# Row-norm deviations as exp(-0.5*ln(v)) on ScalarE, weights centred once, norm steps and their neighbours moved

## What is computed

```python
def _layernorm(x, axis=-1, eps=1e-05):
    m = jnp.mean(x, axis=axis, keepdims=True)
    v = jnp.var(x, axis=axis, keepdims=True)
    return (x - m) / jnp.sqrt(v + eps)
# attention, 16 heads of 8: q = x @ Wq.T + bq, v = x @ Wv.T + bv, buckets from 6 hyperplanes
scores = jnp.einsum('bhsd,bhtd->bhst', q, q) / jnp.sqrt(jnp.float32(E))
same = (b_hs[:, :, :, None] == b_hs[:, :, None, :]).astype(scores.dtype)
attn = jax.nn.softmax(scores * (NB - 2 + same), axis=-1)
# feed-forward, 128 -> 512 -> 512 -> 512 -> 128, ternary weights
h = jax.nn.silu(_tlin(x, w1_w, w1_s)) * _tlin(x, w2_w, w2_s)
h = gelu(_tlin(h, h1_w, h1_s)); h = gelu(_tlin(h, h2_w, h2_s)); return _tlin(h, w3_w, w3_s)
# layer
x = x + _layernorm(attention(_layernorm(x)))
x = x + _layernorm(ffn(_layernorm(x)))
```

## Time and profile before

| | us |
|---|---|
| median of three executions (lowest to highest) | 1383.29 (1378.63 to 1386.29) |
| span of the profiled execution | 1378.0 |
| busy: PE / DVE / ACT / POOL | 1223.5 / 1225.7 / 1084.6 / 1221.7 |
| share of the span: PE / DVE / ACT / POOL | 89% / 89% / 79% / 89% |
| POOL: 128 subtractions L980 | 1138.7 |
| POOL: 48 powers L970 and 48 products L972 | 48.7 and 9.6 |
| ACT: 512 exponentials L1032 | 509.0 |
| ACT: 196 table loads (L1032 88, L1150 31, L1155 31, L1160 29, L1127 16, L1025 1) | 251.5 |
| mean granted clock of TensorE | 0.975 |

### The profile page before, as it was taken

The page is one execution under the profiler, slowest core; times in us unless marked ns, Lnnn a source line. Parts: engine busy times, 40 slices in busy tenths (PEclk is TensorE's granted clock), DMA queues, the critical chain, the costliest instruction groups (busy, mean ns, idle before and its releaser), DMA issues. The chain is left out here.

```text
span 1378.0 us, 19641 instructions
## 1 busy us (share of the span) xinstructions
PE 1223.5 (89%) x5302; PEld 500.2 (36%) x5394; DVE 1225.7 (89%) x3837; ACT 1084.6 (79%) x1573; POOL 1221.7 (89%) x259
## 2 busy tenths in 40 slices
PE   3666799999989999998989999998999999898897
PEld 1211234343333434333343434433343433333343
DVE  4988999999999999999999999999999999999420
ACT  2344778979797988979798897979798897979852
POOL 2699999999999999999999999999999998999810
PEclk9877999999999999999999999999999999999998
DMA  3563445444544455455544544454454535453100
GB/s 104 154 182 112 132 111 154 127 130 120 147 120 118 132 134 141 109 140 125 131 133 124 142 123 132 133 139 129 114 136 128 145 98 146 120 135 102 40 8 8
DMA packets 89470, 167.37 MB, mean 121 GB/s; under 512 B 18192, under 2 KB 54160, under 8 KB 89360
## 3 DMA queue, kind: packets, MB, share of 16 engines
q1 hardware_dynamic: 89252, 165.82, 44.6%
q10 hardware_dynamic: 108, 0.30, 0.1%
HBM read 150.59 MB, written 15.47 MB: 121 GB/s over the span
## 5 line engine op out<-in xcount | busy, mean ns | idle before, releaser
L980 POOL TENSOR_TENSOR logits<-max_row,logits 128x4096 f32<-128x4096 f32 x128 | 1138.7, 8915 | 65.6 <-DMA max_row<-max_scratch 41.0
L808 DVE CUSTOM_DVE_ANT_0 logits<-s_bank,coeff 128x512 f32<-128x512 f32 x1024 | 692.5, 676 | 0.0
L1032 ACT ACTIVATE logits<-logits 128x1024 f32<-128x1024 f32 x512 | 509.0, 1048 | 44.8 <-POOL logits L980 43.6
L758 DVE TENSOR_SCALAR coeff<-brow,bcol 128x516 bf16<-128x516 bf16 x1024 | 485.2, 474 | 36.8 <-PE s_bank L550 31.2
L550 PE MATMUL s_bank<-mov_stack,stat_stack 128*128 128x512 bf16 x932 | 324.8, 393 | 42.4 <-DVE rowmax L808 31.7
L570 PE MATMUL aux_bank<-logits,v_pad 128*32 128x512 f32 x2048 | 255.3, 618 | 39.8 <-ACT logits L1032 38.9
L701 PE MATMUL f_bank<-hid_b,h_sb 128*128 128x512 f32 x512 | 249.0, 594 | 0.9
L690 PE MATMUL f_bank<-hid_a,h_sb 128*128 128x512 f32 x512 | 246.1, 592 | 0.1
L550 PEld LDWEIGHTS s_bank<-mov_stack,stat_stack 128*128 128x128 bf16 x1024 | 93.2, 99 | 317.7 <-DVE rowmax L808 177.8
L690 PEld LDWEIGHTS f_bank<-hid_a,h_sb 128*128 128x128 f32 x512 | 96.0, 190 | 80.6 <-issue 69.3
L701 PEld LDWEIGHTS f_bank<-hid_b,h_sb 128*128 128x128 f32 x512 | 95.0, 190 | 80.8 <-issue 70.9
(11 more groups left out here) (101 smaller groups left out, 911.5 us busy)
## 6 DMA issues: line engine op xcount, KB each, us to landing
max_row<-max_scratch SPq DMA_DIRECT2D x128, 512.0 KB, 4.2
brow<-bucket_scratch SPq DMA_DIRECT2D x63, 522.0 KB, 6.3
mov_stack<-q_scratch SPq DMA_DIRECT2D x192, 96.0 KB
stat_stack<-q_scratch SPq DMA_DIRECT2D x189, 96.0 KB
max_scratch<-rowmax_T SPq DMA_DIRECT2D x512, 1.0 KB
q_scratch<-q_parts SPq DMA_DIRECT2D x16, 384.0 KB, 4.6
x_in<-in_x SPq DMA_DIRECT2D x16, 256.0 KB, 3.1
q_scratch<-q_parts SPq DMA_DIRECT2D x16, 256.0 KB, 5.1
```

Of the source, the lines that this page charges most:

```text
L758: nc.vector.tensor_scalar(coeff[:, k % 3, :].rearrange("p (r n) -> p r n", r=ROW_RUNS), brow[:, h // 4 % 2, h % 4, :, 0:RUN], bcol[:, b % ...
L808: nc.vector.tensor_tensor_reduce(out=logits[:, ring(b, k), :], in0=tile_bank(k)[:], in1=coeff[:, k % 3, 0:SEQ], scale=float(E) ** -0.5, sc ...
L980: nc.gpsimd.tensor_tensor(tiles, max_row[:, m % 2].unsqueeze(2).broadcast_to([P, GROUP, ST, SEQ]), tiles, ALU.subtract).then_inc(below_max ...
L1032: nc.scalar.activation(logits[:, first:first + 2, :], logits[:, first:first + 2, :], ACT.Exp, scale=-1.0).then_inc(probs_done, 1)
```

## The change

The reciprocal deviations of all four norms come from ACT, as exp(-0.5*ln(v + eps)), and the table that is named for both functions takes the place of the softmax's exp table; it is loaded by an instruction of its own behind each pair of Silu or Gelu. POOL's powers and products, `Sqrt` and DVE's reciprocal go. The means of x and y aren't subtracted any more: Wq, Wv, W1 and W2 are multiplied once by I - 1/128 on PE and copied back by ACT. The norm of the attention's output keeps its mean, and its bias is made on DVE in slot 29. Slots move. The diff, cut to its core:

```diff
@@ -54,6 +54,8 @@
 PADDED = ROW_RUNS * RUN
 ROW_PITCH = ROW_RUNS * RUN_PITCH
 EPS = 1e-5
+CONSTS = 5
+EXP_LOG_TABLE = "natural_log_exp_and_others"
...
 SILU_SLOTS = (42, 48)
-MULTIPLY_SLOTS = (48, 48, 52, 52)
-OUTPUT_SLOTS = (100, 101, 104, 104)
+MULTIPLY_SLOTS = (45, 48, 52, 52)
+OUTPUT_SLOTS = (100, 103, 105, 105)
...
 PV_LAGS = (36, 36, 38, 38)
-COPY_LAG = 35
+COPY_LAG = 34
...
 LATE_X_STATS_SLOT = 33
-X_MOMENTS_SLOT = 24
+X_MOMENTS_SLOT = 21
 LATE_X_MOMENTS_SLOT = 37
-X_PREPARE_SLOT = 26
+X_PREPARE_SLOT = 25
 LATE_X_PREPARE_SLOT = 38
-X_RSTD_SLOT = 40
-LATE_X_RSTD_SLOT = 47
...
 XNT_COPY_SLOT = 53
-XNT_SLOT = 57
+XNT_SLOT = 58
 Q_COPY_SLOT = 57
-Q_SLOT = 59
+Q_SLOT = 61
 
-V_SLOT = 32
+V_SLOT = 33
...
 PROJ_SLOT = 25
-BITS_SLOT = 26
+BITS_SLOT = 25
...
 ATT_MOMENTS_SLOT = 25
 ATT_PREPARE_SLOT = 27
-ATT_RSTD_SLOT = 32
-ATT_NORM_SLOT = 31
+ATT_BIAS_SLOT = 29
+ATT_NORM_SLOT = 29
 RESIDUAL_SLOT = 32
-Y1_STATS_SLOT = 32
-Y1_MOMENTS_SLOT = 32
+Y1_STATS_SLOT = 33
+Y1_MOMENTS_SLOT = 34
 Y1_PREPARE_SLOT = 34
-Y1_RSTD_SLOT = 39
-Y1_NORM_SLOT = 37
+Y1_NORM_SLOT = 34
...
 END_PREPARE_SLOT = 49
-END_RSTD_SLOT = 56
 END_NORM_SLOT = 55
-Y2_SLOT = 62
+Y2_SLOT = 61
...
 FFN_LOAD_STEP = 3
-X_RES_SLOT = 44
+X_RES_SLOT = 46
...
+        centre = hid_b[:, 0, 0:P]
...
-            pe.wait_ge(consts_made, 4)
+            pe.wait_ge(consts_made, CONSTS)
+
+            for n, weights in enumerate((wq_sb, wv_sb)):
+                nc.tensor.matmul(f_bank[n][:, 0:E], centre, weights[:], start=True, stop=True).then_inc(centred_psum, 1)
...
                     last.then_inc(xnT_psum, 1)
                 if k == Q_SLOT:
                     pe.wait_ge(xnT_done, p + 1)
+                    if not begun(p):
+                        pe.wait_ge(projection_centred, 2)
                     nc.tensor.matmul(aux_bank[:], wq_sb[:], xnT[:], start=True, stop=True).then_inc(q_psum, 1)
...
                             pe.wait_ge(ynT_done, f + 1)
+                            if f == 0:
+                                pe.wait_ge(ffn_centred, 2)
...
                     pe.wait_ge(ffn_in, 16 * FFN_DMAS)
+                    pe.wait_ge(brow_done, i + 1)
+                    for n, weights in enumerate((w1_sb, w2_sb)):
+                        nc.tensor.matmul(f_bank[n][:], centre, weights[:], start=True,
+                                         stop=True).then_inc(ffn_centred_psum, 1)
...
+                if k == ATT_BIAS_SLOT:
+                    dve.wait_ge(att_rstd_done, f + 1)
+                    nc.vector.scalar_tensor_tensor(out=att_bias[:], in0=att_mv[:, :, 0], scalar=-1.0, in1=att_rstd[:],
+                                                   op0=ALU.mult, op1=ALU.mult).then_inc(att_bias_done, 1)
...
-            def finish_step(g, k):
-                if k == END_RSTD_SLOT:
-                    dve.wait_ge(end_std_done, g + 1)
-                    nc.vector.reciprocal(end_rstd[:], end_std[:]).then_inc(end_rstd_done, 1)
...
-            nc.gpsimd.memset(minus_half[:], -0.5).then_inc(consts_made, 1)
+            nc.gpsimd.memset(centre, -1.0 / E).then_inc(consts_made, 1)
             nc.gpsimd.memset(eps[:], EPS).then_inc(consts_made, 1)
-            pool.wait_ge(consts_made, 1)
+            pool.wait_ge(consts_made, 3)
             nc.gpsimd.affine_select(out=ident[:], in_=ident[:], compare_op=ALU.not_equal, fill=1.0, base=0,
                                     pattern=[[-1, P]], channel_multiplier=1).then_inc(consts_made, 1)
-            pool.wait_ge(consts_made, 4)
-            def rstd(var, shift, out_, bias, prepared, done, bias_done, n):
-
-                pool.wait_ge(prepared, n)
-                nc.gpsimd.tensor_tensor(out_[:], var[:], minus_half[:], ALU.pow).then_inc(done, 1)
-                pool.wait_ge(done, n)
-                nc.gpsimd.tensor_tensor(bias[:], shift[:], out_[:], ALU.mult).then_inc(bias_done, 1)
-
+            nc.gpsimd.affine_select(out=centre, in_=centre, compare_op=ALU.not_equal, fill=1.0 - 1.0 / E, base=0,
+                                    pattern=[[-1, P]], channel_multiplier=1).then_inc(consts_made, 1)
             def subtract(b, m):
 
                 pool.wait_ge(maxima_loaded[m % 2], 16 * (b * GROUPS // 2 + m // 2 + 1))
@@ -997,12 +1000,6 @@
...
-                    if query and k == x_slot(i + 2, X_RSTD_SLOT, LATE_X_RSTD_SLOT):
-                        rstd(x_var, x_shift, x_rstd, x_bias, x_var_done, x_rstd_done, x_bias_done, p + 2)
-                    if feed and k == ATT_RSTD_SLOT:
-                        rstd(att_var, att_shift, att_rstd, att_bias, att_var_done, att_rstd_done, att_bias_done, 2 * f + 1)
-                    if feed and k == Y1_RSTD_SLOT:
-                        rstd(att_var, att_shift, att_rstd, att_bias, att_var_done, att_rstd_done, att_bias_done, 2 * f + 2)
...
-            act.wait_ge(consts_made, 4)
-            nc.scalar.activation(table_warm[:], ident[:, 0:1], ACT.Exp)
+            nc.scalar.preload_act_table_set(EXP_LOG_TABLE)
+            act.wait_ge(consts_made, CONSTS)
             act.wait_ge(projection_in, 16 * PROJECTION_DMAS)
+            for n, weights in enumerate((wq_sb, wv_sb)):
+                act.wait_ge(centred_psum, n + 1)
+                nc.scalar.copy(weights[:], f_bank[n][:, 0:E]).then_inc(projection_centred, 1)
...
-            def prepare(mv, var, shift, ready, done, n):
-
-                act.wait_ge(ready, n)
-                nc.scalar.activation(var[:], mv[:, :, 1], ACT.Identity, bias=eps[:])
-                nc.scalar.activation(shift[:], mv[:, :, 0], ACT.Identity, scale=-1.0).then_inc(done, 1)
-
-            def normalise(dst, src, rstd, bias, done):
+            def rstd(var, scale, log, out_, ready, count, log_done, done, n):
+
+                act.wait_ge(ready, count)
+                nc.scalar.activation(log[:], var, ACT.Ln, bias=eps[:], scale=scale).then_inc(log_done, 1)
+                act.wait_ge(log_done, n)
+                nc.scalar.activation(out_[:], log[:], ACT.Exp, scale=-0.5).then_inc(done, 1)
+
+            def scale_rows(dst, src, rstd_, rstd_done, n, done):
+                act.wait_ge(rstd_done, n)
                 for t in range(ST):
-                    last = nc.scalar.activation(dst[:, t, :], src[:, t, :], ACT.Identity, bias=bias[:, t:t + 1],
-                                                scale=rstd[:, t:t + 1])
+                    last = nc.scalar.activation(dst[:, t, :], src[:, t, :], ACT.Identity, scale=rstd_[:, t:t + 1])
...
                 if k == x_slot(p, X_PREPARE_SLOT, LATE_X_PREPARE_SLOT):
-                    prepare(x_mv, x_var, x_shift, x_mv_done, x_var_done, p + 1)
+                    rstd(x_mv[:, :, 1], 1.0, x_log, x_rstd, x_mv_done, p + 1, x_log_done, x_rstd_done, p + 1)
                 if k == X_NORM_SLOT:
-                    act.wait_ge(x_bias_done, p + 1)
-                    normalise(x_in, x_in, x_rstd, x_bias, xn_done)
+                    scale_rows(x_in, x_in, x_rstd, x_rstd_done, p + 1, xn_done)
...
                 if slot == ATT_PREPARE_SLOT:
-                    prepare(att_mv, att_var, att_shift, att_mv_done, att_var_done, 2 * f + 1)
+                    rstd(att_mv[:, :, 1], 1.0, att_log, att_rstd, att_mv_done, 2 * f + 1, att_log_done, att_rstd_done, f + 1)
                 if slot == Y1_PREPARE_SLOT:
-                    prepare(att_mv, att_var, att_shift, att_mv_done, att_var_done, 2 * f + 2)
+                    rstd(att_mv[:, :, 1], 1.0, y1_log, y1_rstd, att_mv_done, 2 * f + 2, y1_log_done, y1_rstd_done, f + 1)
...
                 if slot == END_PREPARE_SLOT + TILES:
-                    act.wait_ge(end_square_done, (f + 1) * ST)
-                    nc.scalar.activation(end_std[:], end_sum[:], ACT.Sqrt, bias=eps[:],
-                                         scale=1.0 / E).then_inc(end_std_done, 1)
+                    rstd(end_sum[:], 1.0 / E, end_log, end_rstd, end_square_done, (f + 1) * ST, end_log_done, end_rstd_done,
+                         f + 1)
                 if slot == ATT_NORM_SLOT:
                     if f:
 
                         act.wait_ge(h2_done, (f - 1) * HT + 2)
-                    act.wait_ge(att_bias_done, 2 * f + 1)
-                    normalise(f_bank[OUTPUT_BANK][:].rearrange("p (t e) -> p t e", t=ST), att, att_rstd, att_bias, normed_done)
+                    act.wait_ge(att_bias_done, f + 1)
+                    for t in range(ST):
+                        last = nc.scalar.activation(f_bank[OUTPUT_BANK][:, t * E:(t + 1) * E], att[:, t, :], ACT.Identity,
+                                                    bias=att_bias[:, t:t + 1], scale=att_rstd[:, t:t + 1])
+                    last.then_inc(normed_done, 1)
                 if slot == Y1_NORM_SLOT:
-                    act.wait_ge(att_bias_done, 2 * f + 2)
-                    normalise(x_res, y1[:, f % 2], att_rstd, att_bias, yn_done)
+                    scale_rows(x_res, y1[:, f % 2], y1_rstd, y1_rstd_done, f + 1, yn_done)
                 if slot == END_NORM_SLOT + TILES:
```

(37 more changed lines are left out.)

## The result

The changed kernel takes 1446.6 us (median of 4 runs, 1438.8 to 1471.1); the kernel before 1382.5 us (4 runs). The changed kernel's run of 1471.1 us was in a slower state of the chip and is left out of the ratio. The ratio is 1.0438, with an interval of 1.0390 to 1.0487: 4.4% slower, where the prediction had 0.6% faster and a range up to 1387. The profiled execution of the changed kernel spans 1441.8 us, 63.8 more than the 1378.0 of before.

What follows compares the result with a forecast made beforehand. It took DVE as nearest to the bound. Fourteen passes of 0.55 us (7.7) plus 1.0 in the last batch gave 8.7, so 1383.3 - 8.7 = 1374.6 us; own range 1369 to 1379, overall range 1361 to 1387.

Steps and rivals of the forecast that it cites:

- Reciprocal out, bias product in: both 128x4, no difference: On DVE: swapping the reciprocal for the new bias product of equal size was taken to cost nothing.
- so I charge 0: DVE's new wait for att_rstd in slot 29: taken as covered, 0; 0.5 us a pass if that cover goes.
- Rival D: DVE's first product, three slots earlier behind Silu, waits too long and lengthens each pass: 1392 us, chance 0.08.
- rival E: Compiler adds its own table loads, two between bucket rows and Silu, delaying DVE's products: 1404 us, chance 0.05.
- the load inside ACT's wait for the rows: Exponential's table load (1.28 us) moves into ACT's wait before the bucket rows' copy, delaying that copy by 0.15 us.
- PE has the same work ahead of them as before: PE's transposes ahead of `ynT` stay in place, so `ynT` and Silu start only 0.6 us earlier; bounds 0 and 1.36.
- 5 or 6: Expected sign: POOL's wait for maxima grows to this many us a pass, from 2.6.
- 0.3 to 0.6: Expected sign: us a pass that DVE waits for ACT ahead of its first product, no longer ahead of the third.
- Rival C: No change: PE holds the transposes, or DVE's new wait in slot 45 eats the gain; 1381 us, chance 0.22.
- rival B: POOL gated the passes; waits for y, Silu, up branch and some for scores go: 20 us gained, 1363, chance 0.15.
- the last batch's 1.0: After the last accumulator: Ln and Exp save 1.2 us, table loads between Silu pairs lose 0.2; net 1.0 saved.
- DVE is nearest to the bound: Of the engines in a pass, DVE limits most: busy 76.2 of 78.7 us, waiting 2.5 us a pass.

Runs made afterwards that it cites:

- e1: Changed kernel with slot 29's bias product written as four 128x1 products of one tensor and a pointer scalar; 1361.1 us, ratio 0.9876 to the kernel before.
- e3: Kernel before plus one unread dummy 128x4 DVE product a pass in slot 32, first tensor in PSUM, other in SBUF; 1381.4 us, ratio 1.0015.
- e2: Kernel before plus one unread dummy 128x4 DVE product a pass in slot 32, both tensors in SBUF; 1467.2 us, ratio 1.0642.
- e10: e1 with the exp and log table load moved from behind the last Gelu pair to behind the bucket rows' copy; 1373.7 us, ratio 0.9942.
- e12: Kernel before with only the exponential's table load moved directly behind a pass's last Gelu pair, ahead of ACT's wait; 1368.5 us, ratio 0.9916.
- e6: e1 with the output matmuls back in their old slots 100, 101, 104, 104; 1360.4 us, ratio 0.9854 to the kernel before.
- e7: e1 with three pairs of power and product a pass put back on POOL, on constants, read by nobody; 1364.9 us, ratio 0.9888.
- e5: e1 with the first product of gate and up branch back in slot 48; 1362.4 us, ratio 0.9866 to the kernel before.
- e8: Changed kernel with the attention norm's bias made on ACT (negated mean, four 128x1 products), nothing of it on DVE; 1372.6 us, ratio 0.9937.
- e4: Changed kernel with each POOL subtraction cut into two instructions of 128x2048; 1398.9 us, ratio 1.0159 to the kernel before.

## Why the prediction was wrong

**The step that failed** is the one on DVE: "Reciprocal out, bias product in: both 128x4, no difference", and with it "so I charge 0" for slot 29. The product was sized by its elements. The trace of before has no DVE instruction with two SBUF tensors: its sums and products read one of theirs from PSUM. So the operation was one that the trace did not show, and it was to be bounded from both sides. The length that turned out to be the upper bound was in the same trace, POOL's subtraction of 8.9 us, with POOL busy 95% of the pass; but no row of before shows that DVE can be held by it, only e1 to e3 do. Sixteen stalls of up to 8.9 give up to 142 us; the 10 that came cost 78.8 (changed kernel against e1). How many came and how long they were owes to luck, to where slot 29 happens to fall: if the product fell anywhere in a subtraction, the mean stall would be 4.4 us; here it is 8.3, since slot 29 mostly falls on its first microsecond. The description ahead of the prediction says that the engines "meet only at semaphores"; e1 to e3 show that DVE and POOL also meet at SBUF, with no semaphore between them (5.58 us in the median of e2's 16 products, 0.16 in e3). The slower rivals, D and E, were other mechanisms, and neither happened.

**The cause of the sign is thus shown** from three sides: taken out of the changed kernel (e1), put alone into the kernel before (e2), and with a tensor moved to PSUM (e3).

**The gain that the prediction was about** is there once the stall is out: 1378.0 - 1363.0 = 15.0 us between the profiled spans, where 8.7 were forecast. The mechanism, the load inside ACT's wait for the rows, was right (e10 and e12) and a term was too small. The 14 passes went from 78.85 to 77.85 us (marks of e1: 184.2 to 1274.1), so 1.0 each and not 0.55; the rest after the last mark shrank from 90.1 to 88.9, 1.2 against the predicted 1.0. The term is the start of PE's transposes, which the prediction left at 631.36 because "PE has the same work ahead of them as before". But what ended PE's idle time there was ACT's norm of y, which in the kernel before ended at 631.30, 0.06 ahead of them:

```profile
629.67 1.63 ACT L1043 ACTIVATE x_res<-y,att_bias,att_rstd 128x128 f32<-128x128 f32 x4
```

This norm stands behind the table load, so it moves with it. ACT and PE in pass 7 of e1 (compare), and PE in pass 7 of e12:

```profile
619.20 1.28 ACT L1164 ACT_TABLE_LOAD   x1
620.50 0.43 ACT L1097 CAST brow<-f_bank 16x344 bf16<-16x344 f32 x1
...
626.41 0.59 ACT L1145 COPY ynT<-f_bank 128x512 f32<-128x512 f32 x1
...
630.43 1.26 ACT L1150 ACTIVATE hid_a<-f_bank,scales_sb 128x512 f32<-128x512 f32 x2
```

```profile
625.73 0.60 PE L649 MATMUL f_bank<-ident,x_res 128*128 128x128 f32 x4
```

```profile
625.41 0.60 PE L643 MATMUL f_bank<-ident,x_res 128*128 128x128 f32 x4
```

Counted from the end of the last exponential of the group before (621.81 before, 616.61 in e1, 616.20 in e12), in e1 the copy of the rows came 0.17 later, as predicted (0.15). The transposes came after 9.12 us and not 9.55, 0.43 earlier, where I had left them in place; `ynT` after 9.80 and not 10.82, and Silu after 13.82 and not 14.84, 1.02 earlier. (The medians of 13 passes are the same within 0.02.) In e1 the norm ends 2.9 us ahead of the transposes, and PE's own queue holds them. Other kernels split the 0.43. In e12, which changes the load's place alone, the transposes come after 9.22 us, 0.33 earlier, and Silu after 13.87: nearly the whole step. In e6, where the output matmuls stand in their old slots 37 and 40, they also come after 9.22, so moving these matmuls gave the other 0.09. In e10, with the load back behind the copy, the transposes come after 9.13 but Silu after 14.74: there ACT itself reaches `ynT` late.

**Point by point, the rest.** POOL's busy time fell by 55 us for the 60 predicted (pairs 1.25 us each), and e7 shows no cost of it in the time. Its wait for maxima in e1 is 71.8 us in 14 passes, 5.1 a pass, against "5 or 6". DVE waits for ACT ahead of its first product for 7.6 us in 14 waits, 0.54 each, against "0.3 to 0.6". There are 12 table loads a pass and one at the start, so rival E is refuted. DVE does wait in slot 29 for att_rstd, which by the prediction's own sign makes its charge of 0 wrong, but it is 2.6 us in 3 waits in e1, 0.2 a pass. Ln and Exp take 0.3 and 0.2 us, the norms 390 ns for 486, and the exponentials from the new table 1048 ns, as from the old one. Rival C, that the moved product eats the gain, is refuted by e5: back in slot 48 it gives the same time. Rival D did not occur. Two sums of the prediction are off by about 1 us, without weight: rival B's terms, 17.1, 3 and 1, make 21 and not 20, and fourteen passes of 0.15 with the last batch's 1.0 end the forecast's range at 1380 and not 1379. The two copies at the start take 0.27 us each (e1), where the prediction had them at 0.39 at least.

"DVE is nearest to the bound" was half right. In the stall each microsecond of DVE was one of the kernel. But e8 takes work from DVE, gives it to ACT and loses 8 us against e1, and e10 loses 9 by a load on ACT. This fits a loop through ACT, PE and DVE, as the chain from the bucket rows to the products had it, and not one engine; that this loop alone sets the pass is argued and not shown.

## What to carry to other kernels

Size a new instruction not only by its elements, but by where each operand lies and by what POOL is doing in SBUF at that moment: a DVE instruction with two SBUF tensors beside long POOL instructions can cost one of these each time, 8 us for 0.16 here. Write it with a pointer scalar (four of 128x1, 214 ns each at most in e1), or keep one operand in PSUM (164 ns at most in e3). Ask of an idle gap ahead of an instruction what ended it before you say that its own engine holds it. And look for a table load behind an instruction that waits: moving the load into that wait (one line) gave 0.8% here, while the slots that were moved back and the POOL work put back changed nothing that could be told.

## What the runs showed of the hardware

The stall of a DVE instruction by a POOL instruction stands in the profile as busy time of the DVE instruction (85.9 us for 16 of 128x4), not as a wait. It is found by a median far from the minimum of one group, here 8407 against 156 ns. In the changed kernel each stall ends about 20 ns after POOL's instruction, but in e4 one lasted across two POOL instructions that stood one behind the other (8.86 us over halves of 4.5).

A table load takes 1283 ns on ACT. In the kernel before, all 196 stand where ACT goes from one of exponential, Silu, Gelu and `Sqrt` to another, or at the start; copies and Identity between them bring none. No gap stands behind the loads shown here: the exponential starts at 627.76 and its load ends at 627.75; in e12 the copy of the bucket rows starts at 620.09 and the load ends at 620.07.
